# Node slots of a 16-batch attention network on one core: where the last exponentials, the last norm's statistics and root, and two late input norms stand in the order of the engines

## What is computed

```python
x = x + gla_and_mlp(layernorm(x))                 # block 1
y = layernorm(x)                                  # block 2 starts: "late input norm"
nodes = {-1: y}
for c in range(6):                                # six nodes, a graph with fixed sources
    q = ew[c,0]*(nodes[in_q] @ We[eq] + be[eq]);  k, v alike from their own sources
    o = mha(q, k, v, Wq[c], Wk[c], Wv[c], Wo[c])  # 8 heads of 16, 256 x 256 softmax, per batch
    nodes[c] = act_w[c]*o + q
x = x + layernorm(nodes[5]) * g + b               # "last norm", one per batch
```

## Time and profile before

| | |
|---|---|
| median of 3 runs | 1149.46 us (1149.21 to 1154.02) |
| the profiled execution | 1153.58 us, of it the span 1151.8 us |
| mean granted TensorE clock | 0.985 of full speed |
| busy share of the span: PE, PEld, DVE, ACT, POOL | 94%, 65%, 73%, 62%, 36% |
| node slots 407 to 645 us, PE busy | 234.25 of 238.00 us at clock 1.00 |

### The profile page before, as it was taken

How to read it: one execution, slowest core, us unless ns; L and a number is a source line. 1 busy time by engine, 2 the same in 40 slices (tenths; PEclk the granted TensorE clock), 3 DMA queues, 4 the chain that set the end, 5 groups by cost and what they waited for, 6 DMA issues and landing times.

```text
span 1151.8 us, 28156 instructions
## 1 busy us (share of the span) xinstructions
PE 1088.2 (94%) x10313; PEld 745.2 (65%) x10313; DVE 845.3 (73%) x1887; ACT 714.4 (62%) x1597; POOL 420.4 (36%) x818
## 2 busy tenths in 40 slices
PE   8989999988999999999999999999999999999995
PEld 3755555555666666676667766666666766676763
DVE  5467888766688777777777799777777777777784
ACT  3445665553666666666666666666666666666664
POOL 3211121122433334333333377633343334333365
PEclk9889999998999999999999999999999999999998
DMA  8000000026666665676677666567666766676640
GB/s 227 1 1 1 1 0 0 1 29 83 93 95 87 88 89 88 97 95 89 89 97 95 87 95 98 98 98 94 91 85 98 96 89 87 98 94 89 88 69 24
DMA packets 83549, 87.02 MB, mean 76 GB/s; under 512 B 11482, under 2 KB 69342, under 8 KB 83422
## 3 DMA queue, kind: packets, MB, share of 16 engines
q1 hardware_dynamic: 81774, 83.17, 49.9%
q0 software_dynamic: 848, 2.11, 0.7%
q10 hardware_dynamic: 800, 0.05, 0.0%
HBM read 6.51 MB, written 2.10 MB: 7 GB/s over the span
## 4 chain that ended last, share of the span: by engine, by line
PE 78%; DVE 7%; POOL 5%; issue 5%; ACT 4%; DMA 1%; ACTq 0%; SPq 0%; POOLq 0%; DVEq 0%
PE bank L1183 68%; PE bank L1546 4%; PE bank L1553 3%; DVE region L1093 2%; ACT region L769 1%; POOL hl L562 1%; DVE region L972 1%; POOL hl L559 1%; PE bank L1519 1%; POOL region L547 1%; DMA cols<-in_L_attn_gnorm_w 1%; DVE region L1006 1%; ACT region L796 1%; POOL region L542 1%; POOL out L618 0%
## 5 line engine op out<-in xcount | busy, mean ns | idle before, releaser
L1093 DVE TENSOR_REDUCE region<-bank 128x2 f32<-128x512 f32 x768 | 493.6, 685 | 193.1 <-PE bank L1183 193.1
L769 ACT ACTIVATE region<-bank 128x512 f32<-128x512 f32 x768 | 407.6, 604 | 173.3 <-PE bank L1183 173.1
L1183 PE MATMUL bank<-st 48*128 48x256 f32 x3072 | 334.5, 331 | 18.8 <-DVE region L1093 8.1
L1183 PEld LDWEIGHTS bank<-st 48*128 48x128 f32 x3072 | 251.3, 189 | 50.3 <-issue 30.0
L559 POOL TENSOR_TENSOR hl<-qk,one_col 128x512 fp32r<-128x512 f32 x96 | 100.1, 1043 | 465.2 <-ACT qk L734 464.9
L1183 PE MATMUL bank<-region 128*32 128x256 f32 (+5 forms) x3586 | 257.3, 377 | 2.7 <-DVE region L932 1.3
L1183 PEld LDWEIGHTS bank<-region 128*32 128x32 f32 (+3 forms) x3586 | 129.1, 115 | 90.9 <-issue 22.1
L1183 PE MATMUL bank<-mst,ones 64*128 64x512 bf16 x768 | 149.9, 387 | 0.9 <-DMA mst<-mrows 0.9
L562 POOL TENSOR_TENSOR hl<-qk,hl 128x512 fp32r<-128x512 f32 x96 | 122.0, 1271 | 7.5
L783 ACT ACTIVATE region<-bank 128x256 f32<-128x256 f32 x96 | 36.9, 384 | 74.0 <-PE bank L1183 74.0
L1183 PEld LDWEIGHTS bank<-mst,ones 64*128 64x128 bf16 x768 | 36.8, 93 | 60.7 <-issue 42.4
(11 more groups left out here) (194 smaller groups left out, 1427.9 us busy)
## 6 DMA issues: line engine op xcount, KB each, us to landing
st<-hl SPq DMA_DIRECT2D x576, 128.0 KB, 4.8
mst<-mrows SPq DMA_DIRECT2D x192, 6.0 KB
out<-xall POOLq DMA_DIRECT2D x15, 128.0 KB, 2.3
xall<-in_L_attn_hidden_states SPq DMA_DIRECT2D x1, 768.0 KB, 7.1
cst<-in_constants SPq DMA_DIRECT2D x1, 514.5 KB, 4.1
xT<-in_L_ffn_Wq SPq DMA_DIRECT2D x1, 384.0 KB
xT<-in_L_ffn_Wk SPq DMA_DIRECT2D x1, 384.0 KB
xT<-in_L_ffn_Wv SPq DMA_DIRECT2D x1, 384.0 KB
```

The costliest lines, as they stand in the source:

```text
L769: act.activation(to, x_bank(x, k, e)[:, :].rearrange("p (j q) -> p j q", j=2), ACT.Exp).then_inc(B["exp_ok"], 1)
L1093: dve.tensor_reduce(mx[s.n % 2][:, to:to + 2], s_bank(s, k, e)[:, :].rearrange("p (j k) -> p j k", j=2), AX_X, ALU.max, negate=True).then_ ...
L1183: return pe.matmul(o, w, x, start=start, stop=stop, skip_group_check=skip)
```

## The change

On ACT the exponentials of the last x unit go ahead of the values' copy; the last norm's inverse root goes from the end of its z slot to the begin of the next slot, where its step is w. On DVE the last norm's statistics and the two operations of `final_norm` go the same way, from between the maxima of unit 2 and unit 3 to the head of the next slot. The two late input norms are spread over more slots: two tiles of statistics in slot t, two in t+1, moments in t+2, root and two tiles of scaling in t+3, the other two in t+4, and transposes and copy in t+6 (before: 4 tiles in t, moments t+1, root and 4 tiles t+2, transposes t+4).

```diff
@@ ACT phase
                 if z is not None and not z.last:
                     copy_node(z)
+                if w is not None and w.last:
+                    inverse_root(fve, fr, w.f, "fve_ok", "frl", "fra", B)
                 if x is not None:
                     exps(x, 0)
-                if t - 4 in TAILS:
-                    copy_xT(TAILS[t - 4], IN)
+                if t - 6 in TAILS:
+                    copy_xT(TAILS[t - 6], IN)
                 if w is not None and w.last:
                     final_rows(w)
                 if x is not None:
                     exps(x, 1)
-                if t - 2 in TAILS:
-                    inverse_root(ve3, rr3, TAILS[t - 2], "ve3_ok", "r3l", "r3a")
+                if t - 3 in TAILS:
+                    inverse_root(ve3, rr3, TAILS[t - 3], "ve3_ok", "r3l", "r3a")
...
                 if d is not None:
                     copy_ctxT(d)
+                if x is not None:
+                    exps(x, 3)
                 if m is not None:
                     copy_vals(m)
-                if x is not None:
-                    exps(x, 3)
-                if z is not None and z.last:
-                    inverse_root(fve, fr, z.f, "fve_ok", "frl", "fra", B)
@@ DVE
-            def x1_stats(j):
+            def x1_stats(j, tiles=range(TPI)):
...
-                for t in range(TPI):
+                for t in tiles:
                     n = dve.bn_stats(st2[:, t, :], xall[:, ds(TPI * j + t, 1), :])
-                n.then_inc(A["bn2"].sem, 1)
+                if t == TPI - 1:
+                    n.then_inc(A["bn2"].sem, 1)
...
-            def x1_norm(j):
+            def x1_norm(j, tiles=range(TPI)):
                 newton(dve, ve3, rr3, rt3, j, "r3a", "r3b", "r3c", "rstd3_ok")
                 dve.wait_ge(A["rstd3_ok"].sem, A["rstd3_ok"].at(j))
-                for t in range(TPI):
+                x1_rows(j, tiles)
+
+            def x1_rows(j, tiles):
+                for t in tiles:
                     n = dve.tensor_scalar(x1n[:, t, :], xall[...], mv2[:, 0, t:t + 1], rr3[:, t:t + 1], ...)
-                n.then_inc(A["xn2_ok"], 1)
+                if t == TPI - 1:
+                    n.then_inc(A["xn2_ok"], 1)
@@ DVE phase
+                if w is not None and w.last:
+                    final_stats(w)
+                    final_norm(dve, w)
                 if z is not None and z.last:
                     final_sum(z)
...
                 if s is not None:
                     maxes(s, 2, (1,))
-                if z is not None and z.last:
-                    final_stats(z)
-                    final_norm(dve, z)
                 if s is not None:
                     maxes(s, 3)
                 if t in TAILS:
-                    x1_stats(TAILS[t])
+                    x1_stats(TAILS[t], (0, 1))
                 if t - 1 in TAILS:
-                    x1_moments(TAILS[t - 1])
+                    x1_stats(TAILS[t - 1], (2, 3))
                 if t - 2 in TAILS:
-                    x1_norm(TAILS[t - 2])
+                    x1_moments(TAILS[t - 2])
+                if t - 3 in TAILS:
+                    x1_norm(TAILS[t - 3], (0, 1))
+                if t - 4 in TAILS:
+                    x1_rows(TAILS[t - 4], (2, 3))
@@ PE phase
                 burst((0,), (0, 1))
-                if t - 4 in TAILS:
+                if t - 6 in TAILS:
                     pe.wait_ge(B["vals_ok"], m.n)
-                    transpose_x1(TAILS[t - 4], IN)
+                    transpose_x1(TAILS[t - 6], IN)
                 if d is not None:
                     pv(d)
-                if t - 4 in TAILS:
-                    pe.wait_ge(A["xT_ok"], TAILS[t - 4] + 1)
+                if t - 6 in TAILS:
+                    pe.wait_ge(A["xT_ok"], TAILS[t - 6] + 1)
```

## The result

The changed kernel takes 1123.22 us (median of 4 runs, 1121.50 to 1125.43) where the kernel before took 1151.74 on the same chip (4 runs): a ratio of 0.9754, interval 0.9721 to 0.9787. The forecast was 1126.9, so it holds, 3.7 us too high. That it came so close is in part luck: it started from 1149.46, the median of three runs, and the four runs have 1151.74. The change is worth 28.5 us between the medians, where 22.6 were forecast. The profiled executions differ by more, 1153.58 - 1121.50 = 32.1 us. Some 2.1 us of that lie before slot 5, in a part that the change doesn't touch and that differs more than that from run to run (`copy_rows` of slot 5 comes at 288.7 to 294.0 us in the traces of this case). So I count from slot 5 on.

A forecast was written before the change was run, and what follows sets the result against it. PE, seemingly full, was taken to stall at s0 for ACT's exponentials, and POOL's round to bound last-norm slots. -23.5 + 0 + 0.5 + 0.4 = -22.6 us gave 1131.0 profiled, 1126.9 median; own range 1121 to 1132, stated range 1118 to 1138 (0.75).

The forecast's parts named there:

- The hole is the wait for the exponentials: Steady slots, weight loads ahead of s0: the 0.29 us idle listed as issue is s0 waiting for x3's exponentials on ACT.
- I take 0.29, the listed row: Steady slots 6 to 46 and 55 to 94: each of 81 gains 0.29 us, 23.5 us in all.
- The upper bound: Steady slots, loads of x0, s0 and s1: at most 0.33 us gained a slot, 26.7 us on the first term.
- Last-norm slots priced at 0: Slots 47 to 54: POOL's 9.67 us round holds them and no step of it is shortened; 0 us, -0.5 to +0.9.
- a sign of being wrong: Last-norm slots: the prediction would be wrong if they left 9.67 us.
- Another named sign: POOL: the prediction would be wrong if L425 started after an idle wait for ACT.
- Late norms: Late input norms' slots: two tails are 2.0 us over 8.55 where 1.7 over 8.84, giving back 0.5 us for the two.
- The end: Slots 97 on: final_stats and L418 ahead of final_sum cost 0.5 us, slot 97 gains some 0.1; together +0.4 us.
- Another wait takes the place: At s0 or pv: DVE, copy_node or the stack due next, so a slot gains 0.1 us, 1142 us; chance 0.08.
- the hole is issue: Ahead of s0: the hole is issue as the profile names it, not the exponentials; 1149 to 1150 us; chance 0.06.
- Freed last-norm slots: Slots 48 to 54, held by s3's maxima alone, fall from 9.67 to 8.55: another 7.8 us, 1119 us; chance 0.07.
- Slower: Last norm: L418 also waits for four small POOL operations, POOL's round grows 0.6 us, +6 us, 1156 us; chance 0.04.

The follow-up runs named there:

- e1: Kernel before with only the exponentials of the last x unit moved ahead of the values' copy on ACT: 1125.31 us, ratio 0.9758.
- e4: Kernel before plus one unread 128x256 ACT copy ahead of the last x unit's exponentials, from slot 6 on: 1176.03 us, ratio 1.0205.
- e5: Changed kernel plus one unread 128x256 ACT copy ahead of the last x unit's exponentials, from slot 6 on: 1123.93 us, single run.
- e6: Changed kernel with L418 and L419 as one-element reductions instead of tensor_scalar, last norm's epsilon left out: 1124.51 us, ratio 0.9747 to the kernel before.
- e7: Changed kernel with the finished batch's DMA started by SP instead of POOL: 1118.93 us, ratio 0.9702 to the kernel before.
- e2: Kernel before with only the last norm's statistics, final_norm and inverse root moved to the head of the next slot: 1153.93 us, ratio 1.0004.

## Why the forecast held, and where it was off

**The hole is the wait for the exponentials: right.** One edit alone takes it away (e1), a dose lengthens it one for one (e4), and in the new order there is room (e5). What I took for the next thing late, the maxima for s1, is not late: PE idles 0.02 us a slot.

**"I take 0.29, the listed row": the step that was mis-sized.** A slot gained 0.38, over 69 plainly steady slots 26.2 us where 20.0 were forecast, which is most of the miss. The hole in the listing begins where x0's last load ends and ends where s0's first begins. It leaves out that loads in an unbroken stream go closer together: twelve `st` loads take 0.89, where four took 0.42 and eight 0.56 apart (e4's rows), 0.98 in all. The missing 0.09 is that. The upper bound failed by the same: "x0, s0 and s1 could take 1.08 where they took 1.41", and they take 1.03, for the third unit was priced at half of 0.56, a price from loads standing apart, and four loads within the unbroken row take (0.89 - 0.42) / 2 = 0.24. The better price was in the trace of before all the same, where x2 and s2 follow one another:

```profile
507.70 0.66 PEld L1183 LDWEIGHTS bank<-st 48*128 48x128 f32 x8
```

Eight in one row take 0.66 where four take 0.42, so one more unit adds 0.24: 0.80 + 0.24 = 1.04 instead of 1.41, or 0.37 a slot. The busy time shows it only afterwards: PE's rows for the same matmuls were 234.25 / 26.9 = 8.70 us a slot, and are 8.44 now.

**Last-norm slots priced at 0: right in what bounds them, wrong that nothing in the round is shortened.** POOL's round holds them (e6, e7), L418 ends with L562, and PE's wait moved from s1 to pv as forecast. But they left 9.67, which the prediction had named as a sign of being wrong; the norm's edit alone does it (9.52 in e2, while e1 stays at 9.67). `split_maxima` had been waiting too. In the kernel before, DVE behind the L418 of the earlier trace rows that took 1.71 us, and POOL behind the L562 of the earlier trace rows:

```profile
672.10 0.16 DVE L419 TENSOR_SCALAR region<-region 128x2 f32<-128x2 f32 x1
672.17 1.28 DVE L1093 TENSOR_REDUCE region<-bank 128x2 f32<-128x512 f32 x2
```

```profile
673.59 0.22 POOL L575 TENSOR_TENSOR mxp<-region,one_col 128x16 bf16<-128x16 f32 x1
```

The maxima of s3, pushed by L418, end at 673.45 and L575 starts at 673.59, 1.36 us after L562's start; after the change it starts 1.23 after it. 0.13 of the 0.15 by which the round fell is this, and it comes off every slot: I had called the round one "without a pause of its own but the wait for `final_rows`", and a pause of 0.08 us without a mark in the row was there (673.51 to 673.59). These slots are -0.7 us of the miss. Another named sign came as well, outside the slots that POOL bounds: L425 waits 0.34 us for ACT's root in slots 97 and 98.

**Late norms: right in the steps, low in the sum.** The rows of DVE around x0 of slots 11, 12 and 13 (337.62, 346.68, 355.89), against the earlier trace rows:

```profile
337.42 0.94 DVE L960 TENSOR_TENSOR region<-region 128x4 f32<-128x4 f32 x1
...
347.86 0.60 DVE L1010 TENSOR_SCALAR region<-xall,region 128x128 f32<-128x128 f32 x2
348.37 2.48 DVE L1098 TENSOR_REDUCE region<-bank 128x2 f32<-128x512 f32 x4
...
356.09 0.88 DVE L1010 TENSOR_SCALAR region<-xall,region 128x128 f32<-128x128 f32 x2
356.88 2.47 DVE L1098 TENSOR_REDUCE region<-bank 128x2 f32<-128x512 f32 x4
```

The first maxima of slot 12 start at x0 + 1.69 (forecast 1.7) and those of slot 13 at x0 + 0.99 (forecast 1.2; x0 + 0.96 is on time). From x0 to x0, slot 11 is over 8.46 by 0.60 (0.5 forecast), slot 12 by 0.75 (0.7), slot 13 by 0.05 (0.2), slot 18 with the transposes by 0.59 (0.6): two tails of 2.0, as forecast. What I had left out is slot 9, 0.36 over: its `normalise` pauses 0.46 us between L1120 and L1124, where it pauses 0.10 in the other slots, and the transposes of ctx wait 0.38 for it. The pause stands in slot 9 of each of the seven kernels with the new late norms and in none of the five with the old; why is open. In sum the ten slots gain 3.8 less 0.9 given back, where 0.5 was forecast. That is no reason against the new order: with the old one and the exponentials' edit (e1) these ten slots give back 1.5 (89.53 where 91.81 - 3.8 = 88.0 was full gain).

**The end: right in the sum,** +0.5 against +0.4. The step from slot 97 to 98 costs more than the 0.5 forecast, 0.75 (8.68 where it took 7.93), and slots 94 to 97 gain 0.25, not 0.1.

**The rivals.** Another wait takes the place: no, the slot gained 0.38; the hole is issue: no, by e4. Freed last-norm slots: no, they keep 9.52; what frees them is the DMA's place (e7). Slower: L418 waited for L562 alone, and POOL's round got shorter.

## What to carry to other kernels

A gap between weight loads on a full-looking engine is a wait when it keeps a constant distance to another engine's end; price it by the unit's time in an unbroken stream, not by the gap's own length. Where a stage is bound by a round on one engine, look in it for starts that are later than the end before them with no mark in the row, and take work off that engine before moving anything else: one DMA issue moved to SP's queue was worth 6 us by the stretches (4.3 between the medians), taking out the port nothing in the changed kernel, and with the issue gone the norm's new place nothing either. Ask of an idle time ahead of an operation whether what follows needs the same thing; if so it stays when the operation goes. Count what an operation moved to the head of a round costs in the last rounds, where nothing covers it.

## What the runs showed of the hardware

- A listed hole of 0.29 us in the weight loads cost 0.38, and 0.26 of the 0.38 was booked as busy PE time.
- A 128x2 `tensor_scalar` on DVE takes 0.17 us alone and up to 1.75 beside POOL's 128x512 operations; the same values by `tensor_reduce` take 0.15 to 0.16 wherever they stand (e6). L418 took 0.17 beside a DMA issue on POOL with nothing behind it (at 1109.98 in the kernel before), so the issue alone did not hold it there.
- A DMA issue on POOL takes 0.79 to 0.81 us; moving it to SP took 0.7 us off the slots that POOL's round held. The 0.29 of waiting ahead of it was for ACT's copy and stayed (0.39 in e7).
- Twelve 48x128 f32 weight loads take 0.89 us in an unbroken stream and 0.98 as four and eight apart.
